# A gated 3x3 convolution on one core: seeds of two tiles and the last set sums moved to TensorE, statistics earlier, VectorE work given to GpSimd and ScalarE

## The reference

```
x: [8, 64, 48, 48]                                        # images, channels, rows, columns
v      = group_norm(x, groups of 2 channels, eps 1e-5)
logits = conv1x1(v, coupler_w) + coupler_b                # 8 filter sets per pixel
sel    = softmax(logits over the 8 sets); sel = sel / sum(sel)
conv   = conv3x3(v, 8 sets of 64 filters, padding 1) + bias
y      = x + sum over s of sel[s] * conv[s]               # [8, 64, 48, 48]
```

## Time and profile before

| | us |
|---|---|
| median of three runs | 336.83 (336.24 to 336.9) |
| profiled execution | 337.13, of which the span 335.3 |
| PE busy | 323.8 (97%) |
| DVE busy | 277.4 (83%) |
| POOL busy | 229.6 (68%) |
| ACT busy | 110.8 (33%) |

### The profile page before, as it was taken

How to read it: one execution, slowest core, us unless ns; L and a number is a source line. 1 busy time by engine, 2 the same in 40 slices (tenths; PEclk the granted TensorE clock), 3 DMA queues, 4 the chain that set the end, 5 groups by cost and what they waited for, 6 DMA issues and landing times.

```text
span 335.3 us, 5416 instructions
## 1 busy us (share of the span) xinstructions
PE 323.8 (97%) x1684; PEld 153.7 (46%) x1684; DVE 277.4 (83%) x499; ACT 110.8 (33%) x167; POOL 229.6 (68%) x329
## 2 busy tenths in 40 slices
PE   8995999999999999999999999999999999999994
PEld 8533344444544444444544444444544444444441
DVE  2799799997799988887799878887799877777786
ACT  1688162175221162175221162175221111111112
POOL 3700696899994698899854788899864788334343
PEclk9999899999999999999999999999999999999999
DMA  6799389009960397019870496009820496010002
GB/s 201 312 264 220 76 209 223 23 2 233 224 192 0 89 239 179 3 33 241 201 173 3 125 227 152 0 30 239 178 57 0 120 236 152 0 42 28 3 1 70
DMA packets 30374, 41.93 MB, mean 125 GB/s; under 512 B 2128, under 2 KB 23248, under 8 KB 29968
## 3 DMA queue, kind: packets, MB, share of 16 engines
q1 hardware_dynamic: 29184, 37.78, 46.7%
q10 hardware_dynamic: 1168, 3.89, 3.9%
HBM read 12.56 MB, written 4.72 MB: 52 GB/s over the span
## 4 chain that ended last, share of the span: by engine, by line
PE 87%; DMA 4%; DVE 3%; POOL 2%; SPq 1%; issue 1%; ACT 1%; DVEq 0%; ACTq 0%
PE pair L397 54%; PE pair L409 18%; PE pair L405 14%; DMA op<-v_tail 2%; DMA x_raw<-x 2%; POOL v_pts L1091 2%; PE side L387 1%; DVE last_mixed L853 1%; DVE v_pts L975 0%; SPq L305 0%; ACT w_head L632 0%; DVE pair L828 0%; DVE half L837 0%; DVE v_tail L987 0%; DVE high L829 0%
## 5 line engine op out<-in xcount | busy, mean ns | idle before, releaser
L397 PE MATMUL pair<-w_head,op 128*128 128x512 f16 x864 | 234.8, 381 | 3.9 <-DMA op<-v_tail 3.8
L397 PEld LDWEIGHTS pair<-w_head,op 128*128 128x128 f16 x864 | 84.1, 98 | 106.0 <-DMA op<-v_tail 4.4
L409 PE MATMUL pair<-w_tail,op 128*128 128x512 f16 x288 | 109.5, 380 | 0.0
L590 ACT ACTIVATE m_sb<-pair 128x512 f32<-128x512 f32 x72 | 42.9, 596 | 196.7 <-PE pair L409 189.2
L1114 POOL TENSOR_TENSOR quarter<-half 128x256 f32<-128x256 f32 x71 | 52.7, 742 | 61.7 <-DVE half L837 60.9
L828 DVE TENSOR_TENSOR pair<-pair,sel_now 128x512 f32<-128x512 f32 x71 | 49.4, 696 | 35.1 <-PE pair L409 34.5
L837 DVE TENSOR_TENSOR half<-pair,high 128x512 f32<-128x512 f32 x71 | 49.1, 692 | 10.2 <-DVE high L829 1.0
L405 PE MATMUL pair<-w_tail,op_two 128*128 128x512 f16 x144 | 55.0, 382 | 0.0
L812 DVE TENSOR_TENSOR pair<-pair,m_sb 128x512 f32<-128x512 f32 x72 | 49.6, 689 | 0.0
L814 DVE TENSOR_TENSOR pair<-m_sb,pair 128x512 f32<-128x512 f32 x72 | 49.3, 684 | 0.0
L829 DVE TENSOR_TENSOR high<-pair,sel_now 128x512 f32<-128x512 f32 x71 | 48.3, 680 | 0.0
(11 more groups left out here) (109 smaller groups left out, 198.8 us busy)
## 6 DMA issues: line engine op xcount, KB each, us to landing
op<-v_head SPq DMA_DIRECT2D x14, 600.0 KB, 8.1
x_res<-x_pix SPq DMA_DIRECT2D x8, 576.0 KB, 6.5
op_two<-v_head SPq DMA_DIRECT2D x14, 300.0 KB, 9.0
op<-v_tail SPq DMA_DIRECT2D x14, 300.0 KB, 6.5
op<-v_head SPq DMA_DIRECT2D x14, 288.0 KB, 8.4
out<-y_out SPq DMA_DIRECT2D x7, 576.0 KB, 4.0
x_raw<-x ACTq DMA_DIRECT2D x3, 1152.0 KB, 10.5
w_raw<-weight SPq DMA_DIRECT2D x3, 768.0 KB, 8.7
```

Of the source, the lines that this page charges most:

```text
L397: nc.tensor.matmul(dst, op[b][:, 0, j, at + r * PW:at + r * PW + P], w_head[:, j, r, :], start=fresh and r == 0, stop=False, skip_group_ch ...
L409: return nc.tensor.matmul(dst, op[b][:, 1, j, at:at + P], w_tail[:, j, 0, :], start=False, stop=True, skip_group_check=True)
L590: act.activation(m1_sb[:, i % LOOK, :], pair[i % SETS_OF_BANKS][:, 0, :], ACT.Copy).then_inc(m1_copied, 1)
```

## The change

- Four constants (bias, coupler weights and biases, the three matrices) come in one DMA on SP; before, ACT issued four small DMAs for three of them.
- POOL's inverse deviation stands ahead of all raw points of the third load. Between them POOL now also makes the filter sums of row 2 (`row_two`), and afterwards the remaining heads of points 0 and 1 (`rest_head`), which ACT made before.
- ACT makes the first head of point 1 ahead of the three `bound_of`, and takes the coupler heads from DVE. The load of the next x (`load_ahead(1)`) and of the residual (`load_res(0, 0)`) are issued later.
- The first fill of points 0 and 1 goes point by point.
- Tiles 0 and 1 need no seeds from DVE: PE computes point 0 into both banks and adds point 1 to the first bank and, from a negated operand (`op_neg`, made by ACT), takes it from the second.
- For tiles 0 to 3 ACT makes the products of the first pixel (`even_products`), DVE those of the second (`multiply_odd`). The weights of the first six tiles are written by one fused operation (`weights_soon`).
- In every round the moments are combined on ACT, not DVE, one tile later.
- The last tile is summed by PE: an identity matrix times the residual and times each of the eight products, 9 f32 matmuls of 64 columns for each pixel of the pair.

```diff
-WARM_SMALL = 28
-WARM_WIDE = 6
+WARM_SMALL = 18
+WARM_MORE = 3
+WARM_WIDE = 4
-SUMS_AT = (3, 3)
-SQUARES_AT = (4, 5)
+SUMS_AT = (4, 4)
+SQUARES_AT = (5, 6)
+EVEN_TILES = 4
+SEEDED = 2
 ...
 # SP
-            first_fill(0, 0)
+            for k in range(2):
+                first_fill_head(k)
+                first_fill_tail(k)
+            first_fill_late()
+            rest_fill(0)
             load_res(0, 0)
-            first_fill(1, 0)
-            first_fill(0, 1)
-            first_fill(1, 1)
+            rest_fill(1)
 ...
 # PE
+            def second_point_less(t, dst):
+                at = t * P
+                for r in range(K):
+                    nc.tensor.matmul(dst, op_neg[:, 0, at + r * PW:at + r * PW + P], w_head[:, 1, r, :],
+                                     start=False, stop=False, skip_group_check=True)
+                return nc.tensor.matmul(dst, op_neg[:, 1, at:at + P], w_tail[:, 1, 0, :],
+                                        start=False, stop=True, skip_group_check=True)
 ...
             for i in range(3):
                 first_point(i, 0, 0, i == 0)
-            for i in range(3):
-                first_point(i, 1, 0, i == 0)
+                if i < SEEDED:
+                    point(0, 0, i, pair[i][:, 1, :], True)
+            pe.wait_ge(first_pt[1], 16 * (F_PARTS + 1))
+            for i in range(SEEDED, 3):
+                first_point(i, 1, 0, i == SEEDED)
             pe.wait_ge(c_tails, 1)
             pe.wait_ge(h_first, 2)
             pe.wait_ge(t_first, 2)
             logits(0)
+            pe.wait_ge(negated, 1)
+            for i in range(SEEDED):
+                point(0, 1, i, pair[i][:, 0, :], False)
+                second_point_less(i, pair[i][:, 1, :]).then_inc(m2_done, 1)
             round_(0, True, True)
 ...
+            pe.wait_ge(xb_done, ROUNDS * 2 * BIAS_PARTS)
+            for a, dst in enumerate((w_bank[:, 0:C], side[:, 0:C])):
+                nc.tensor.matmul(dst, eye_mat, x_res[1][:, TPI - 1, a, :], start=True, stop=False)
+                for k in range(SETS):
+                    pe.wait_ge(last_steps[a], k + 1 if a == 0 else k // (SETS // 2) + 1)
+                    last = nc.tensor.matmul(dst, eye_mat, last_prod[:, a, k, :], start=False, stop=k == SETS - 1)
+                last.then_inc(last_sums, 1)
 ...
 # ACT
+            first_heads(1, 0)
             bound_of(0)
-            first_heads(1, 0)
+            fill_beside(0)
             bound_of(1)
+            fill_beside(1)
             bound_of(2)
-            fill_beside()
 ...
             for r in range(K):
                 w_heads_of(0, slice(r, r + 1))
-            load_ahead(1)
             first_heads(3, 0)
+            coupler_heads()
             w_heads_of(1)
-            first_heads(1, 1)
-            first_heads(0, 1)
             act.activation(w_mix_head[:, :, :], w_mix[:, :, :], ACT.Copy, scale=scale[:, 0:1]).then_inc(w_mix_heads, 1)
+            act.wait_ge(first_pt[1], 16 * (F_PARTS + 1))
+            act.activation(op_neg[:, :, :], op[0][:, :, 1, 0:NEG_COLS], ACT.Copy, scale=-1.0).then_inc(negated, 1)
             w_heads_of(2)
-            copy_m1(0, 0)
             w_heads_of(3)
 ...
+                act.wait_ge(last_sums, 1)
+                act.activation(y_out[1][:, TPI - 1, 0, :], w_bank[:, 0:C], ACT.Copy).then_inc(last_steps[0], 1)
 ...
 # DVE
             first_input_point(0)
-            input_tails_of(1, 0, 1)
             first_head()
             input_tails_of(0, 0, 2)
+            input_tails_of(1, 0, 2)
             first_input_point(1)
+            kernel_point2(0)
             weight_bound()
-            kernel_point2(0)
+            kernel_point2(1)
             scales()
-            kernel_point2(1)
+            input_tails_of(2, 0, 3)
             first_point_tail(0)
             first_point_tail(1)
-            kernel_point2(2)
             first_point_tail(2)
-            input_tails_of(2, 0, 3)
             input_tails_of(3, 0, 4)
+            coupler_tails()
+            input_tails_of(1, 1, 1)
             second_point_tails()
-            coupler_parts()
-            input_tails_of(1, 1, 1)
             input_tails_of(0, 1, 2)
             mixed_tails()
 ...
 # POOL
+            inverse_deviation(0)
+            def row_two():
+                outer = [w_raw[:, 2, kx, :] for kx in (0, 2)]
+                pool.wait_ge(w_loaded[2], 16)
+                pool.tensor_tensor(w_outer, outer[0], outer[1], ALU.add).then_inc(w_row2, 1)
+                pool.wait_ge(w_row2, 1)
+                pool.tensor_tensor(w_pt1[2], w_outer, w_raw[:, 2, 1, :], ALU.add).then_inc(w_row2, 1)
+                pool.tensor_tensor(w_pt2[:, 2, :], w_outer, w_raw[:, 2, 1, :], ALU.subtract).then_inc(w_row2, 1)
 ...
```

More of the change, by code:

```diff
@@ new lines, in first_fill_late @@
+            def first_fill_late():
+                pts, cols, below = slice(2, NP), slice(0, PW + FIRST_PAIRS), slice(0, FIRST_PAIRS)
+                heads = v_head[0:C, pts, :]
+                wait(h_first, NP)
+                sp.dma_start(op[0][0:C, 0, pts, cols], heads[:, :, cols]).then_inc(first_late, 16)
+                sp.dma_start(op[0][0:C, 1, pts, cols], heads[:, :, cols]).then_inc(first_late, 16)
+                sp.dma_start(op[0][C:P, 1, pts, below], heads[:, :, PW:PW + FIRST_PAIRS]).then_inc(first_late, 16)
+                sp.dma_start(op_two[0][0:C, :, cols], heads[:, :, cols]).then_inc(first_late, 16)
+                wait(t_first, NP)
+                sp.dma_start(op[0][C:P, 0, pts, cols], v_tail[0:C, pts, cols]).then_inc(first_late, 16)
@@ L872, in round_ @@
                         dve.wait_ge(sel_rest, 1)
-                    if i + 1 < TILES or more:
+                    if begin and i < EVEN_TILES:
+                        multiply_odd(i)
+                        if i == 0:
+                            divide_again(0, 0)
+                        dve.wait_ge(even_done, i + 1)
+                        halve(i, n)
+                    elif i + 1 < TILES or more:
                         multiply(i, n)
@@ L886, in round_ @@
                         divide(0, 1)
-                    if begin and i == 3:
                         add_up_again(0, 1)
+                    if begin and i == 4:
                         invert_again(0, 1)
@@ L891, in round_ @@
                         selection(0, sel_now_parts, sel_rest, 1)
-                    if more and i == 4:
-                        combine(n + 1)
                     if more and i == 6:
@@ L1201 @@
     matrices = np.stack([0.5 * same_group, eye - 0.5 * same_group, eye], axis=1)
+    coupler = np.zeros((P, 2 * SETS), np.float32)
+    for b in range(2):
+        coupler[C * b:C * b + C, SETS * b:SETS * b + SETS] = np.asarray(L0_conv_coupler_w).reshape(SETS, C).T
+    constants = np.concatenate([matrices.reshape(P, 3 * P), coupler,
+                                np.broadcast_to(np.asarray(L0_conv_coupler_b), (P, SETS)),
+                                np.broadcast_to(np.asarray(L0_conv_bias), (P, C))], axis=1)
     host = {
```

319 lines of the change are left out of this document (191 added, 128 removed).

## The result

| | before | after |
|---|---|---|
| median time, us | 336.85 (336.24 to 336.9, 4 runs) | 340.34 (339.73 to 341.1, 4 runs) |
| profiled execution, us | 337.13, span 335.3 | 341.1, span 339.3 |
| start of tile 3, us | 39.56 | 40.05 |
| tile 3 to PE's last 512-column matmul, us | 290.46 | 292.72 |
| from there to the last store's issue, us | 3.46 | 4.68 |

The ratio is 1.011, 95% interval 1.0093 to 1.0127. The forecast was 336.2, faster. The two profiled executions differ by 3.97 us, and the three stretches by 0.49 + 2.26 + 1.22 = 3.97.

What follows compares the result with a forecast made beforehand. PE was taken as the bound, full from 80 to 330 us, leaving prologue and end to decide: 337.13 - 0.2 (x) - 1.45 (tile 3 sooner) + 1.0 (end) = 336.5 profiled, 336.2 us as median; 8-in-10 range 334.7 to 337.7.

Steps and rivals of the forecast that it cites:

- The stretch from tile 3 to the last point: Rounds behind the prologue: PE is full there, so edits cost nothing; a change above 0.4 us would refute the forecast.
- ACT's products of tile 3: First round: they stand behind the next x's sums and end about 1.2 us late; cost 0 to 0.5, taken 0.
- The clock: Rival, prologue: PE's clock falls in the thin stretch from 16.3 to 22.4 us, losing 1.7 us: 337.9, chance 0.15.
- Start of the statistics: Prologue: POOL is free sooner, so the inverse deviation starts at about 11.37, not 11.97, 0.60 us sooner.
- ACT's small loads: Prologue: dropping ACT's four small DMAs brings x 0.2 us sooner, by engine share; bounds nothing to about 1.5 us.
- PE's mark at 22.45: Prologue: the first tail matmul's start stays, since sooner statistics and a filter scale 0.65 us later cancel.
- the rival of an early x: Rival, prologue: x lands a microsecond sooner because packets count, not engine time: 335.2, chance 0.20.
- POOL is free for the deviation: Prologue: with six raw points ahead POOL is free at 11.23, before DVE's variance at 11.29.
- DVE held by POOL ahead of the logits: Prologue: POOL's two heads delay DVE's tails to 28.3 to 29.5, taken 29.0; tile 0's last points at 33.8.
- The bound of 32.95: Prologue: earliest start of tile 0's last points if PE's own matmuls alone decide; the other end was 34.4.
- the rival in which POOL disturbs nobody: Rival, prologue: DVE is done by 28, tile 0's last points start at 33.0: 335.4, chance 0.10.
- The tail: Behind the last point: 36 small f32 matmul pieces of 0.107 us replace DVE's reductions, 1.0 us later (0.9 to 1.4).

Runs made afterwards that it cites:

- e3: Changed kernel with the remaining weights of the first images and GpSimd's two bias products one tile sooner: 337.4 us, ratio to before 1.0008.
- e5: Changed kernel with ACT's sums and squares of the next x, and the moments' combination, one tile sooner: 339.62 us, ratio to before 1.0071.
- e6: Changed kernel with only GpSimd's two bias products moved back behind tiles 3 and 4, weights still a tile late: 339.94 us, ratio to before 1.0102.
- e4: Changed kernel with ACT's products for three tiles, not four, DVE making all of tile 3's: 338.97 us, ratio to before 1.005.
- e1: Changed kernel with 14 more warming matmuls filling PE's gaps between 18.4 and 22.5 us: 338.14 us, ratio to before 1.0042.
- e2: Changed kernel with the old end, DVE's two reductions in place of the 18 small f32 matmuls and ACT's copy: 339.33 us, ratio to before 1.007.
- b1: Kernel before the change with one load of all constants on SP's queue in place of ACT's four small ones: 335.9 us, ratio 0.9971.
- f2: Changed kernel with the edits of e1, e2, e3, rearranged warming matmuls, row two's third operation behind DVE's scales, logits and input tails sooner: 334.55 us.
- f1: Changed kernel with the edits of e1, e2, e3, plus four warming matmuls ahead of the filter bound and nine in the row behind: 334.43 us.
- c2: Changed kernel with the edits of e1, e2, e3, but five warming matmuls in the row and GpSimd's third row-two operation behind DVE's scales: 334.85 us.

## Why the prediction was wrong, point by point

- **The stretch from tile 3 to the last point, forecast as 0, is the step that failed first: +2.26 us.** I costed the moved combination of moments and DVE's relief, and argued that nothing changes a time under a PE at 250.00 of 250.00. But a full PE only says that every buffer came in time, not by how much. The diff also moved the remaining weights one tile later and GpSimd's two bias products with them, from a place where POOL waited for DVE to one in front of the next image's points. I never walked POOL's queue through round 0. e3 gives 2.6 us back; e5 and e6 exclude the moments and the product's place alone; e4 shows that ACT's products of tile 3, which I counted as 0 to 0.5 and took as 0, cost up to 1.35 as long as the weights are late. The later moments themselves cost nothing in the other rounds: PE has 230.00 of 230.00 us from 100 on, and e3, which keeps them, needs 290.10 us from tile 3 on, less than the 290.46 before.
- **The clock, a rival at 0.15 and 1.7 us, was the likely case.** The trace loses 2.8 us, and all four runs of the kernel after have a mean of 0.984 to 0.990. (The mean alone doesn't show it: most runs of the kernel before lie at 0.988 to 0.995, with the fall at 34 us of the earlier trace rows.) I held against it that no single gap was above 1.8 us and that the earlier trace rows show the fall only behind 3.32. Here it fell with the longest gap 1.37 us, in a stretch in which PE was busy 1.50 of 4 us (18 to 22). The reason against was drawn from one instance in the rows. e1 settles cause and price. That instance I also read too large: of the 2.0 us that I put down to the clock from 33.23 to 39.56, 0.3 was a wait, since DVE's half of tile 0 was ready only at 39.50 and PE's last matmul ahead of tile 3 had started at 39.03. Which of the gaps decides is open: in the profiled runs of e2, e4, e5 and e6, with the same code there, it had fallen by about 18 us, in that of the kernel after at about 21.3.
- **Start of the statistics and ACT's small loads: 0.2 us taken, 2.4 measured** (b1), outside my bounds of 0 to 1.5. The engine share of 4.2% was the wrong measure. ACT's bounds ended at 16.08, 1.7 sooner than the 17.8 of my sum and 0.6 sooner than before; the third filter load, there by 13.96, didn't hold them. It didn't move PE's mark at 22.45, because POOL's operations then held DVE's scales (0.70 and 0.80 us for 0.15 each) and a tail. For that reason the rival of an early x, 335.2, failed too. The step beside it, that POOL is free for the deviation, was right: at 9.72 it has waited 0.76 us for DVE.
- **PE's mark at 22.45 stays: right, 22.51, by luck.** The bounds came 1.7 us sooner than I summed, POOL's hold took 1.2 back at the scales, so that the filter heads start at 18.88 and not at 19.2 to 19.5, and DVE then has a tail that POOL holds, 1.38 us, ahead of its three filter tails. Without the hold at the scales and at full clock f2 has the mark at 20.88.
- **DVE held by POOL ahead of the logits: mis-sized.** I put the logits at 29.0 and the last points of tile 0 at 33.8. At full clock e1 has them at 28.33 and 33.13, f1 at 27.97 and 32.78, and in both the logits follow PE's own matmuls without a wait for DVE: in the kernel after POOL was through at 23.47, and one tail took the hold (22.38, 1.70 us, the next 0.81), not two, and was covered. That I went nearer to the full hold, to 29.0, was my estimate, and no run shows DVE through so late: it had the tail that the logits need at 27.94 in the kernel after, 28.13 in e1 and, the latest, 28.60 in c2. The bound of 32.95 that I worked out for PE alone, and the rival in which POOL disturbs nobody, were the nearer ones here. Without the fall of the clock the head (all up to tile 3) would have gained 2.1 us (39.56 - 37.45 in e1), not 1.45. The hold itself is real: with POOL idle a scale takes 0.15 or 0.16 us (c2), beside it `undo` took 0.70 and `minus_half_scale` 0.80, and in the kernel after `undo` ends at 17.99, where GpSimd's third operation on row two ends at 17.97. The other two of the four took 0.15 each, with POOL at work too; what decides which operation is held is not shown.
- **The tail (the end behind the last point), +1.0 forecast (0.9 to 1.4), +1.22 measured**, at 0.109 us a piece against 0.107. Mechanism and size were right.

Against the forecast for the profiled execution, 336.5, the measured 341.1 is 4.6 more: head 2.15 (40.05 against 37.9 with the early x), rounds 2.26, end 0.22.

## What to carry to other kernels

Walk every in-order queue through the first round when its inputs are moved: work that stood ahead of a wait cost little, and the same work one place later, in front of a chain, cost its whole length (1.93 of the 2.23 us by which POOL's first point came later). Where an edit takes matmuls out of a prologue, look at all the gaps that are left in the stretch, not only at the longest, and fill them. Look where a hold goes before taking it away: here 1.1 us on DVE's scales were lost again where GpSimd's work came to lie beside the next operations of DVE.
